# Moving the last accumulation, changing the PSUM bank of the routed output and giving three residual adds to GpSimd, in the tail of a fused attention and mixture-of-experts layer

## What is computed

```python
xn = _layernorm(x, axis=-1)
s = _L0_attn_ref(xn, L0_attn_WQ, L0_attn_WK, L0_attn_WV)
g = _silu(_L0_ffn_ref(xn, L0_ffn_w_gate, L0_ffn_w1, L0_ffn_w2, L0_ffn_w3, L0_ffn_sw1, L0_ffn_sw2, L0_ffn_sw3, L0_ffn_expert_bias))
x = x + s * g
...
# in _L0_ffn_ref: 8 experts, 2 per token
routed_in = xf[flat_idx]
h = jax.nn.silu(_grouped_mm(routed_in, w1, counts)) * _grouped_mm(routed_in, w3, counts)
routed_out = _grouped_mm(h, w2, counts)
shared = jax.nn.silu(xf @ sw1.T) * (xf @ sw3.T) @ sw2.T
out = shared.at[flat_idx].add(routed_out)
```

## Time and profile before

| | |
|---|---|
| median of 3 runs | 237.82 us (237.39, 237.82, 237.92) |
| profiled execution | 238.74 us, span 236.7 us, mean granted TensorE clock 0.993 |
| TensorE busy | 228.2 us, 96% of the span |
| VectorE, ScalarE, GpSimd busy | 176.6 us (75%), 144.9 us (61%), 55.3 us (23%) |

### The profile page before, as it was taken

How to read it: one execution, slowest core, us unless ns; L and a number is a source line. 1 busy time by engine, 2 the same in 40 slices (tenths; PEclk the granted TensorE clock), 3 DMA queues, 4 the chain that set the end, 5 groups by cost and what they waited for, 6 DMA issues and landing times.

```text
span 236.7 us, 4676 instructions
## 1 busy us (share of the span) xinstructions
PE 228.2 (96%) x1533; PEld 205.6 (87%) x1533; DVE 176.6 (75%) x620; ACT 144.9 (61%) x392; POOL 55.3 (23%) x107
## 2 busy tenths in 40 slices
PE   7899999999999999999999999999999999999983
PEld 5688898998999989989899998898988889898843
DVE  3878669788797888877777875668676867859665
ACT  2454755756557556485575542878778696778722
POOL 5220732706318055091012000002020210202000
PEclk9999999999999999999999979999999999999999
DMA  6599430110200200000000000115847547383522
GB/s 198 186 318 307 150 91 1 29 59 6 89 3 1 88 3 3 0 0 3 0 0 4 0 3 0 48 38 187 178 86 183 91 132 129 100 204 63 131 78 100
DMA packets 18758, 19.45 MB, mean 82 GB/s; under 512 B 1064, under 2 KB 17712, under 8 KB 18736
## 3 DMA queue, kind: packets, MB, share of 16 engines
q1 hardware_dynamic: 15568, 16.02, 21.3%
q0 software_dynamic: 3168, 3.15, 8.8%
HBM read 14.95 MB, written 4.21 MB: 81 GB/s over the span
## 4 chain that ended last, share of the span: by engine, by line
PE 92%; DVE 2%; DMA 1%; ACT 1%; POOL 1%; issue 1%; DVEq 0%; ACTq 0%
PE bank L392 85%; PE bank L484 4%; PE bank L440 3%; DMA x_ring<-in_L_attn_x 1%; DVE raw_sw L1381 1%; POOL rstd L333 1%; DVE w L1379 1%; PE bank L556 1%; PE bank L414 0%; DVE bn L1088 0%; DVE arena L949 0%; ACT xT_hi_all L731 0%; ACT arena L731 0%; ACT probs L731 0%; ACT attn_all L731 0%
## 5 line engine op out<-in xcount | busy, mean ns | idle before, releaser
L392 PE MATMUL bank<-xT_hi_all,arena 128*128 128x512 f32 (+3 forms) x256 | 79.5, 367 | 0.7 <-DVE arena L949 0.7
L392 PE MATMUL bank<-arena 128*128 128x256 f32 (+2 forms) x560 | 76.8, 285 | 0.3 <-ACT attn_all L731 0.3
L392 PEld LDWEIGHTS bank<-arena 128*128 128x128 f32 (+1 forms) x560 | 72.0, 186 | 4.9 <-issue 0.8
L392 PEld LDWEIGHTS bank<-xT_hi_all,arena 128*128 128x128 f32 x256 | 46.8, 189 | 6.8 <-DVE arena L949 0.9
L731 ACT ACTIVATE arena<-bank 128x512 fp32r<-128x512 f32 (+4 forms) x84 | 36.2, 453 | 26.8 <-PE bank L392 25.2
L949 DVE TENSOR_TENSOR arena<-bank,arena 128x264 fp32r<-128x264 f32 (+4 forms) x83 | 41.5, 509 | 15.0 <-ACT arena L731 14.7
L392 PE MATMUL bank<-xT_lo_all,arena 128*128 128x512 f32 (+3 forms) x128 | 45.8, 358 | 0.0
L383 POOL DMA_DIRECT2D x_ring<-in_L_attn_x x6 | 7.9, 1316 | 79.0 <-DVE x_ring L1317 79.0
L392 PEld LDWEIGHTS bank<-xT_lo_all,arena 128*128 128x128 f32 x128 | 24.2, 189 | 2.2
L731 ACT ACTIVATE attn_all<-bank,row_inv 128x256 f32<-128x256 f32 x32 | 15.2, 474 | 16.4 <-PE bank L392 15.6
L761 ACT ACTIVATE probs<-bank,neg_max 128x128 f32<-128x128 f32 (+3 forms) x32 | 17.0, 530 | 9.5 <-DVE neg_max L1007 9.4
(11 more groups left out here) (127 smaller groups left out, 368.3 us busy)
## 6 DMA issues: line engine op xcount, KB each, us to landing
x_ring<-in_L_attn_x SPq DMA_DIRECT2D x7, 512.0 KB, 3.5
x_ring<-in_L_attn_x POOLq DMA_DIRECT2D x6, 512.0 KB, 5.8
out<-x_ring SPq DMA_DIRECT2D x6, 512.0 KB, 3.3
spread<-pairs SPq DMA_DIRECT2D x14, 128.0 KB, 3.1
w_sb<-in_L_ffn_w SPq DMA_DIRECT2D x1, 1024.0 KB, 10.9
raw_sw<-in_L_ffn_sw SPq DMA_DIRECT2D x3, 256.0 KB, 4.5
x_ring<-in_L_attn_x SPq DMA_DIRECT2D x2, 256.0 KB, 2.9
xn<-in_L_attn_x SPq DMA_DIRECT2D x1, 512.0 KB, 5.5
```

The costliest lines, as they stand in the source:

```text
L392: return nc.tensor.matmul(dst, lhsT, rhs, start=start, stop=stop, skip_group_check=True, **kw)
```

## The change

There are four edits. `accumulate(7, 1)` stands ahead of `shared_out(6, 1)` on TensorE, and on ScalarE and VectorE `rows_high(7, 1)` and `rows_low(7, 1)` stand ahead of `silu_out(6, 0)` and `gate_attn(6, 0)`. The routed output and tile 0 go to bank 0 (`h1_bank[0]`) instead of bank 4, with a wait for `h_mult_done` in place of the one for `gate_done`. GpSimd adds x in the tiles 0, 1 and 2. VectorE adds it in tile 3 after all four multiplications.

```diff
@@ gpsimd, after the six add_x
+            pool.wait_ge(s["x7_loaded"], 16)
+            for t in range(T - 1):
+                pool.wait_ge(s["last_gated"], t + 1)
+                nc.gpsimd.tensor_tensor(x_last[:, t, :], x_last[:, t, :], gate[:, t, :], ALU.add).then_inc(s["last_summed"], 1)
@@ sync
             for t in range(T):
-                sp.wait_ge(s["last_summed"], t + 1)
+                sp.wait_ge(*((s["last_summed"], t + 1) if t < T - 1 else (s["final_summed"], 1)))
@@ tensor, routed_out: o_bank becomes h1_bank[0] in both matmuls
@@ tensor, last step
             accumulate(i, 0)
+            accumulate(i, 1)
             shared_out(i - 1, 1)
-            accumulate(i, 1)
+            pe.wait_ge(s["h_mult_done"], C * B - 1)
             pe.wait_ge(s["sum_ready"], 1)
             nc.tensor.transpose(bc_bank[:, 0:PAIRS], sum_w[0:PAIRS, :], ident[0:PAIRS, 0:PAIRS]).then_inc(s["sum_turned"], 1)
-            pe.wait_ge(s["gate_done"], 2 * i)
             routed_out()
...
-            for t, dst in enumerate((o_bank, acc_bank, g_bank, bc_bank)):
+            for t, dst in enumerate((h1_bank[0], acc_bank, g_bank, bc_bank)):
@@ scalar, last step
             silu_rows(i, 1)
+            rows_high(i, 1)
             silu_out(i - 1, 0)
-            rows_high(i, 1)
             silu_hidden(i, 1)
@@ vector, last step
             rows_low(i, 0)
+            rows_low(i, 1)
             gate_attn(i - 1, 0).then_inc(s["gated"], 1)
-            rows_low(i, 1)
             h_mult(i, 1)
...
-                dve.wait_ge(s["last_gated"], t + 1)
-                nc.vector.tensor_tensor(x_last[:, t, :], x_last[:, t, :], gate[:, t, :], ALU.add).then_inc(s["last_summed"], 1)
+            dve.wait_ge(s["last_gated"], T)
+            nc.vector.tensor_tensor(x_last[:, T - 1, :], x_last[:, T - 1, :], gate[:, T - 1, :], ALU.add).then_inc(s["final_summed"], 1)
```

More of the change, by code:

```diff
@@ L196, in build @@
             bc_done one_hot_done gathered rows_silu rows_hi rows_lo pair_one_hot_done accumulated0 accumulated1
-            inv_part wqk_loaded sum_ready sum_turned pairs_ready last_tile_done last_gate_done last_gated x6_loaded x7_loaded added6 stored6 x0_hi x0_lo x0_turned gate_loaded x0_part x0_stats x0_var x0_rstd pairs_turned pairs_kept pairs_out spread0 spread1 last_summed bias_loaded""".split()
+            inv_part wqk_loaded sum_ready sum_turned pairs_ready last_tile_done last_gate_done last_gated x6_loaded x7_loaded added6 stored6 x0_hi x0_lo x0_turned gate_loaded x0_part x0_stats x0_var x0_rstd pairs_turned pairs_kept pairs_out spread0 spread1 last_summed final_summed bias_loaded""".split()
         s = {n: sem(n) for n in names}
@@ L603, in routed_out @@
             def routed_out():
-                mm(o_bank[:, 0:D], zero_bf[:, 0:P], zero_bf[:, :], True, False)
+                mm(h1_bank[0][:, 0:D], zero_bf[:, 0:P], zero_bf[:, :], True, False)
                 pe.wait_ge(s["pairs_ready"], 1)
                 for g in range(E):
-                    mm(o_bank[0:8, 0:D], pair_out[:, g * 8:(g + 1) * 8], w2_sb[:, g, :], False, False)
+                    mm(h1_bank[0][0:8, 0:D], pair_out[:, g * 8:(g + 1) * 8], w2_sb[:, g, :], False, False)
             def out_tile(t, dst, onto=False):
@@ L620, in shared_out @@
                 for u in range(2):
-                    ins = out_tile(2 * half + u, o_bank[:, u * D:(u + 1) * D], onto=i == B - 1 and u == 0)
+                    ins = out_tile(2 * half + u, o_bank[:, u * D:(u + 1) * D], onto=False)
                 ins.then_inc(s["o_done"], 1)
@@ L937, in _ @@
             h_high(i, 1)
-            for t, src in enumerate((o_bank, acc_bank, g_bank, bc_bank)):
+            for t, src in enumerate((h1_bank[0], acc_bank, g_bank, bc_bank)):
                 act.wait_ge(s["last_tile_done"], t + 1)
```

## The result

The changed kernel is slower by a third of a per cent: 238.13 us (median of 22 runs) against 237.45 for the kernel before (22 runs, with the three shown above among them). The ratio is 1.0032, with a 95% interval of 1.0016 to 1.0048, so 0.4 to 1.1 us. The prediction had 237.9 us, in 237.3 to 238.4, and gave a loss of over 0.2% a chance of 0.20.

A forecast was written before the change was run, and what follows sets the result against it. In the last 17 us TensorE was taken to wait before the transpose and VectorE to bound the final tiles. With 0.13 us won in front, the net was put at +0.05 on 237.82, forecasting 237.9 us, range 237.3 to 238.4.

The forecast's parts named there:

- no change could be told: Whole kernel: a difference within 0.2% (0.48 us) of the kernel before, given a chance of 0.62.
- wrong upwards: Last tiles: the prediction fails this way if adds take over 0.85 us or the last add itself waits for GpSimd.
- The front's new wait: TensorE, between the two groups of 4 matmuls: a new gap of 0.61 us, waiting for VectorE's `rows_low`.
- 0.13 us are won: Front: after 16 matmuls in 1.89 us the transpose comes at 225.40 instead of 225.53.
- ends 0.28 behind GpSimd: Last tiles: a 128x256 VectorE operation with both inputs in SBUF is held until 0.28 us after GpSimd's operation.
- VectorE is not held: Last tiles: larger operations might interleave with GpSimd's, -0.43 us in sum, 237.4 us; chance 0.20.
- The add of 0.61 us: Last tiles: estimated time of a 128x256 add on GpSimd, under the 0.72 us of a tile, so GpSimd keeps up.
- I take +0.05, near the first of the two: Net effect chosen between -0.02 us (only VectorE held) and +0.23 us (GpSimd held as well).
- The second of the two computed courses: Last tiles: VectorE holds GpSimd as well, tile 3's store goes +0.36 us later; less 0.13, +0.23 us.
- +0.24 (below): Net sum if the Trainium skill's rule holds in both directions; by the trace's rows alone it was put at -0.04.
- may add up to 0.25: Last stores: tile stores only 0.34 us apart, each keeping the DMA engines busy for 0.6 us, may cost this much.
- The other bank saves nothing by itself: Routed output: bank 0 gains nothing alone; in bank 4 the zeroing matmul would wait for `silu_out(6, 1)` until 226.2.

The follow-up runs named there:

- e10: e1 without the transpose's wait for the hidden multiplication; ratio to the kernel before 0.9998, front 7.27 us.
- e1: Changed kernel with the tail's edits taken back, leaving the moved accumulation and bank 0; ratio to the kernel before 1.0005, front 7.26 us, tail 5.14 us.
- e3: Changed kernel with the last tiles' silu and last product left in PSUM, GpSimd's adds kept; ratio to the kernel before 1.0000, tail 4.98 us.
- e8: e1 with the routed output back in bank 4 and its wait for the silu; ratio to the kernel before 1.0019, front 7.65 us.
- e2: Kernel before with only GpSimd's adds of x in three of the last tiles; ratio to the kernel before 1.0035, tail 5.71 us.

## Why the prediction was right and where it was not

The measured 238.13 lies in the range, and that is luck in part. The forecast of 237.9 stood on a median of 237.82 from three runs; 22 runs gave 237.45, which is 0.37 lower, while the change cost 0.68 us by the medians instead of about 0.1. The two errors cancel for the most part. Put on 237.45, the same forecast is about 237.5 with a range up to 238.0, and 238.13 is outside. The forecast that most likely no change could be told does not hold: a loss of over 0.2%, which came, was given 0.20. The prediction's own signs for "wrong upwards" came too: one add took 0.90, and the last add itself waited for GpSimd. Step by step:

- **The front's new wait: right.** The prediction had TensorE going on 0.61 us after the end of `accumulate(7, 0)`; counted in issues it is 222.64 - 221.56 - 4 x 0.118 = 0.61. VectorE's reduction was covered, the late hidden layer stayed hidden.
- **"0.13 us are won": the size was off.** 0.01 was lost. The 16 matmuls and the transpose took 224.68 - 222.64 = 2.04 us where the prediction had 1.89. Of the 0.15, 0.05 are the first matmul after the wait (the next one starts 0.17 later instead of 0.12), and 0.09 lie before the transpose. e10 shows that the second wait isn't the reason; the reason stays open. e1 shows the front to be neutral as a whole.
- **A VectorE operation with two SBUF inputs is held and ends 0.28 behind GpSimd: right,** three times to 0.01 us, though the rows were of 128x32 and the 0.28 an estimate. e3 settles that it is the operands: one of them in PSUM, and nothing is held. The prediction's case that VectorE is not held (0.20) is out.
- **The add of 0.61 us: the term was too small.** Undisturbed it takes 0.71 to 0.73 (e3), and it starts 0.15 us after VectorE's operation, where 0.05 was taken from another pair of engines (add 1 starts 0.08 after its multiplication). So it doesn't keep up with 0.72 a tile comfortably.
- **"I take +0.05, near the first of the two, because the trace has never shown GpSimd stretched": this step failed.** It is why a change of about nothing was forecast and 0.6 us were lost. The second of the two computed courses, in which VectorE holds GpSimd, is the one that came. It had the last store's issue start 0.36 us later; the trace has 0.48 (234.10 - 228.81 = 5.29 against 234.48 - 229.67 = 4.81), and the issue itself took 0.43 us instead of 0.33. An estimate from the rows gives the share of the stretched adds: with add 1 and add 2 at 0.72 and VectorE still held by them, the last add would end near 233.7 instead of 233.97. So about 0.3 of its 0.38 come from GpSimd being held, and 0.1 from the add's size and late start.
- **The premise of that step was not true either.** The trace before does have one stretched add. L358 is a 128x32 operation on GpSimd, eight times; seven start with no VectorE operation of two SBUF inputs running, and one, at 128.79, starts 0.02 us behind such an operation:

```profile
L358 POOL TENSOR_TENSOR raw_qkv<-raw_qkv,bias_bc x8: 251/252/280, 30.5 to 128.8; 128x32 f32<-128x32 f32 x8
...
128.77 0.18 DVE L1057 TENSOR_TENSOR raw_qkv<-raw_qkv 128x32 f32<-128x32 f32 x1
128.79 0.28 POOL L358 TENSOR_TENSOR raw_qkv<-raw_qkv,bias_bc 128x32 f32<-128x32 f32 x1
```

  It takes 0.280 where the others take 0.25. That is one case of 0.03 us; VectorE's operations of this kind were too short to show more. The 12 operations of 128x512 that the prediction went by show no hold, but nothing long with two SBUF inputs runs on VectorE when they start.
- **The comparison with the Trainium skill.** The prediction has "+0.24 (below)" and "-0.04" there, but the courses below give +0.23 and -0.02; the forecast went by the latter. The Trainium skill ("SBUF — State Buffer", "Who interferes with whom") says that the two engines' shared access is an exclusive lock, and that the one that issues first keeps the other out for its whole instruction. Both directions agree with the changed kernel's trace. "Fully out", as the prediction puts it, is a little too much: a held multiplication of 0.42 us ends 0.28 behind GpSimd, and a held add of 0.72 ends 0.58 behind VectorE, so about 0.14 us of each ran before the other was done.
- **Stores closer together "may add up to 0.25": nothing was added.** A store lands 1.7 us after its issue in both kernels (medians), and the span ends 1.9 us after the last issue in both.
- **The other bank saves nothing by itself and avoids a wait: right.** In e8 the zeroing matmul starts 0.76 us behind the transpose, where the prediction had the silu end 0.8 behind it. The price of 0.39 us had not been worked out there, and was put too low (0.1 to 0.3) for e8.

The sum in the end: front +0.01, tail +0.58, together 0.59 us by the traces, within the 0.4 to 1.1 of the runs. That the loss is nearly all GpSimd's is shown by e1 and e2; how the remainder up to the median difference of 0.68 comes about is within the scatter of the runs.

## What to carry to other kernels

Work moved from VectorE to GpSimd did not pay here while both engines' operations read two operands from SBUF: three adds of 0.42 us became 0.73 to 0.90 on GpSimd, and three of VectorE's operations went from 0.42 to 0.70 to 0.94. With one operand of VectorE's work left in PSUM they ran side by side, and the move paid 0.16 us. When a trace shows one engine held by another, ask in which direction the rows could have shown it: no long case is not the same as no hold. When a wait is removed by moving its producer forward, compute when the producer's own inputs are ready, and put just enough other work in front (here 6 matmuls of 12): that turned a neutral move into 0.43 us.

## What the runs showed that I had not expected

After 15.5 us of idling a GpSimd operation started 0.15 us after the VectorE operation that it waits for (230.75 to 230.90), three times what VectorE to TensorE takes (0.05); after 0.36 us of idling it was 0.08 (231.91 to 231.99). An fp32 transpose behind split matmuls started 0.21 us after the last one in e1 and e10, against 0.12 between the matmuls, with one wait or two. SyncE's fourth store took 0.43 us to issue when it followed the third directly (changed kernel, e3), 0.33 in the kernel before, where the issues are apart.
